# Dense query and key projections spread by transfers, maxima in a ring of three banks, and a schedule with one long piece to a slot

## The reference

```python
def _L1_attn_ref(x, w_qkv, b_qkv, w_proj, b_proj):
    ...
    q, k, v = (qkv[0], qkv[1], qkv[2])
    attn = jnp.einsum('bhqd,bhkd->bhqk', q, k) * SCALE
    attn = jax.nn.softmax(attn, axis=-1)
    out = jnp.einsum('bhqk,bhkd->bhqd', attn, v)
    ...
t = t + _L1_attn_ref(_ln_t(t), L1_attn_w_qkv, L1_attn_b_qkv, L1_attn_w_proj, L1_attn_b_proj)
t = t + _L1_ffn_ref(_ln_t(t), ...)
```

## Time and profile before

| | |
|---|---|
| Time, median of 3 runs | 249.68 us (248.03 to 251.86) |
| Profiled execution, its own time | 250.09 us |
| Its span | 248.2 us, mean granted clock 0.989 |
| PE, DVE, ACT, POOL busy | 229.0, 149.8, 118.0, 71.8 us |

### The profile page before, as it was taken

The page is one execution under the profiler, slowest core; times in us unless marked ns, Lnnn a source line. Parts: engine busy times, 40 slices in busy tenths (PEclk is TensorE's granted clock), DMA queues, the critical chain, the costliest instruction groups (busy, mean ns, idle before and its releaser), DMA issues.

```text
span 248.2 us, 5871 instructions
## 1 busy us (share of the span) xinstructions
PE 229.0 (92%) x2020; PEld 149.0 (60%) x2020; DVE 149.8 (60%) x330; ACT 118.0 (48%) x210; POOL 71.8 (29%) x117
## 2 busy tenths in 40 slices
PE   2999997989999999999889989999999999998982
PEld 2989874555557667667575564555555565644371
DVE  0129567557677678696765837566656656555183
ACT  0345056354543463463544336575756657565312
POOL 8000007000001800814510231574555546542000
PEclk9999999999999999999997999999999999999998
...
GB/s 189 228 108 121 245 276 367 358 256 248 246 81 3 3 31 0 3 33 3 198 155 0 4 46 16 49 49 50 48 48 48 48 63 48 45 51 18 93 181 127
DMA packets 25187, 25.95 MB, mean 105 GB/s; under 512 B 5900, under 2 KB 23884, under 8 KB 25164
## 3 DMA queue, kind: packets, MB, share of 16 engines
...
...
## 4 chain that ended last, share of the span: by engine, by line
PE 82%; DVE 8%; ACT 4%; DMA 3%; issue 2%; POOLq 0%
PE grid L1423 11%; PE grid L1195 9%; PE bank L1451 9%; PE grid L1430 7%; PE bank L1132 4%; PE bank L1439 4%; PE bank L1229 3%; PE bank L1211 3%; PE bank L1088 3%; PE grid L1040 3%; PE grid L1327 3%; PE bank L1135 3%; PE grid L1168 2%; PE grid L1332 2%; PE bank L1341 2%
## 5 line engine op out<-in xcount | busy, mean ns | idle before, releaser
L679 ACT ACTIVATE main<-down_all 128x576 f32 x42 | 28.5, 684 | 26.9 <-PE bank L1451 25.9
L974 DVE COPY main<-main 128x1152 f32 x41 | 31.6, 771 | 16.0 <-issue 14.1
L788 DVE TENSOR_REDUCE main<-grid 128x4 f32<-128x1024 f32 x24 | 29.3, 1223 | 18.0 <-PE grid L1168 18.0
L648 ACT ACTIVATE main<-grid 128x1024 f32<-128x1024 f32 x24 | 24.5, 1024 | 25.3 <-PE grid L1195 25.3
L517 POOL DMA_INDIRECT main<-xhat_rows,main x21 | 22.8, 1087 | 30.1 <-PE bank L1411 17.1
L1423 PE MATMUL grid<-main 128*64 128x384 f32 x160 | 29.7, 488 | 0.3 <-DVE main L958 0.3
L525 POOL DMA_INDIRECT pair_rows<-main x19 | 20.4, 1073 | 28.6 <-DVE main L964 28.6
L1168 PE MATMUL grid<-main 32*128 32x256 f32 x192 | 26.2, 400 | 1.1 <-ACT main L606 1.1
L1195 PE MATMUL grid<-main 32*128 32x256 f32 x192 | 26.1, 400 | 0.2 <-ACT main L648 0.2
L1451 PEld LDWEIGHTS bank<-main 128*64 128x64 f32 x228 | 16.1, 136 | 12.2 <-ACT main L679 8.9
L1451 PE MATMUL bank<-main 128*64 128x192 f32 x228 | 22.7, 333 | 0.0
...
## 6 DMA issues: line engine op xcount, KB each, us to landing
down_all<-wd SPq DMA_DIRECT2D x16, 288.0 KB, 4.8
...
```

The source lines that it names most:

```text
L648: act.activation(probs[:, quad % 2, 2 * (n % 2):2 * (n % 2) + 2, :, :].rearrange("p h k n -> p h (k n)"), grid[:, score_banks(n), :], ACT. ...
L679: act.activation(w_dn[:, p, h, :], dn_e(expert(t, h)), ACT.Copy).then_inc(S["w_dn_ready"], 1)
L788: vec.tensor_reduce(negmax[:, g % QUADS, :, col:col + 33:32].rearrange("p q h -> p h q"), grid[:, max_banks(n), :].rearrange("p h (q n) -> ...
L974: vec.tensor_copy(w_gu[:, p, h, :], gu_e(expert(t, h))).then_inc(S["w_gu_ready"], 1)
```

## The change

- Queries and keys of all quads but the first are projected densely: 64 columns of queries and 64 of keys in one result of 128 partitions, two quads at a time (`project_pair`). ACT evicts each into `dense`, and SP copies the rows by transfers to the even partitions of `qk_sb` (`spread_rows`), two transfers for each quad. Users wait with `wait_spread`. POOL fills the odd partitions once. The scale moves to the exponential.
- The raw weights are loaded in the dense layout, in eight transfers of short pieces, and only the first quad's are spread by DVE.
- The maxima have a ring of three banks (2, 3, 4), one bank for each head. `maxima` takes one head at a time.
- `maxima_rows` stands behind the scores of the odd slot. The second dense result and half of the values lie in bank 5 beside it, and PE waits for `shift_ready` before it writes there.
- The long pieces have slots of their own: `DENSE_AT`, `VALUES_AT`, `OUT_AT`, `TOKENS_AT`, `LOGITS_AT`.
- Expert weights are loaded in groups of experts, between the steps of `spread_rows`.

```diff
+SHIFT_ROW = 1
+WQ = 3 * 2 * C + 3 * C
+DENSE_AT = (None, 0, 3, 7, 13, 16)
+VALUES_AT = (5, 11, 17)
+OUT_AT = (9, 15, 19)
+TOKENS_AT = (14, 20)
+LOGITS_AT = (18, 21)
+RING = (2, 3, 4)
+GU_GROUPS = ((0, 3), (3, 5), (5, 8), (8, 11), (11, 13), (13, 16))
+DN_GROUPS = ((0, 4), (4, 8), (8, 12), (12, 16))
+LD_GU = 16 * 4 * len(GU_GROUPS)
+LD_DN = 16 * len(DN_GROUPS)
...
-        def out_slot(b):
-            return UNITS * (b + 1) + (1 if b == B - 2 else 2)
-        def max_banks(n):
-            i = 0 if n == 0 else 2
-            return slice(i, i + 2)
+        def max_bank(n, h):
+            return bank[h if n == 0 else RING[(2 * n + h - 2) % 3]]
         def score_banks(n):
             i = 2 if n == SPAN - 2 else 0
             return slice(i, i + 2)
-        def query_bank(m):
-            return bank[5 if m == 1 else 4][:, 0:N]
-        def key_bank(m):
-            return bank[6 if m in (1, 2) else 7][:, 0:N]
+        def dense_quads(p):
+            return [m for m in (2 * p + 1, 2 * p + 2) if m < B * QUADS]
+        def dense_bank(p, form):
+            if p == 0:
+                return bank[(5, 6)[form]][:, 0:N]
+            return bank[5][:, N:2 * N] if form else bank[7][:, 0:N]
+        def wait_spread(engine, m):
+            p = (m - 1) // 2
+            copies = sum(2 * len(dense_quads(c)) for c in range(p % 2, p + 1, 2))
+            engine.wait_ge(spread_qk[p % 2], 16 * copies)
         def value_bank(h):
-            return bank[4 if h else 7][:, 0:C]
+            return bank[5][:, N:N + C] if h else bank[7][:, 0:C]
...
-            sp.dma_start(w_raw[:, 0, :], a["w_qkv"][0:128, 0:C]).then_inc(S["ld_qkv"], 16)
-            sp.dma_start(w_raw[:, 1, :], a["w_qkv"][C - 128:C, C:2 * C]).then_inc(S["ld_qkv"], 16)
-            sp.dma_start(w_raw[64:128, 2, :], a["w_qkv"][128:C, 0:C]).then_inc(S["ld_qkv"], 16)
-            sp.dma_start(w_raw[0:64, 2, :], a["w_qkv"][0:C - 128, C:2 * C]).then_inc(S["ld_qkv"], 16)
+            for rows, m, start in ((slice(0, 128), 0, 0), (slice(0, 128), 1, C - 128), (slice(64, 128), 2, 128), (slice(0, 64), 2, 0)):
+                for part in range(2):
+                    sp.dma_start(w_d[rows, m, :, part, :], a["w_qkv"][start:start + rows.stop - rows.start, part * C:(part + 1) * C]
+                                 .rearrange("p (j n) -> p j n", j=QUADS)).then_inc(S["ld_qkv"], 16)
...
+                for part in range(2):
+                    sp.dma_start(first_bias[0:128:2, part:part + 1], a["b_qkv"][part * C:part * C + 64].unsqueeze(1)).then_inc(S["ld_qkv"], 16)
+                    sp.dma_start(dense_bias[64 * part:64 * part + 64, :],
+                                 a["b_qkv"][part * C:(part + 1) * C].rearrange("(j r) -> r j", j=QUADS)).then_inc(S["ld_qkv"], 16)
                 for r in range(4):
-                    sp.dma_start(qk_bias[32 * r:32 * r + HD, :],
-                                 a["b_qkv"][0:2 * C].rearrange("(j r d) -> r d j", r=4, d=HD)[r]).then_inc(S["ld_qkv"], 16)
...
+            def spread_rows(p):
+                for form, m in enumerate(dense_quads(p)):
+                    sp.wait_ge(S["dense_ready"], 2 * p + form + 1)
+                    if p == 0:
+                        sp.wait_ge(S["odd_rows_set"], 2)
+                    if m >= 2 * QUADS:
+                        sp.wait_ge(S["st_done"], 2 * (m - 2 * QUADS) + 2)
+                    for part in range(2):
+                        sp.dma_start(qk_sb[0:128:2, m % (2 * QUADS), part, :],
+                                     dense[64 * part:64 * part + 64, p % 2, form, :]).then_inc(spread_qk[p % 2], 16)
+            load_gate_up(*GU_GROUPS[0])
+            load_down(*DN_GROUPS[0])
+            spread_rows(0)
             sp.wait_ge(S["tok_ready"], B)
-            for e in range(BEFORE, E - LATE):
-                load_expert(e, S["ld_late"])
+            load_down(*DN_GROUPS[1])
+            load_gate_up(*GU_GROUPS[1])
+            spread_rows(1)
+            load_gate_up(*GU_GROUPS[2])
+            spread_rows(2)
+            load_gate_up(*GU_GROUPS[3])
+            spread_rows(3)
+            load_gate_up(*GU_GROUPS[4])
+            load_down(*DN_GROUPS[2])
+            spread_rows(4)
+            load_down(*DN_GROUPS[3])
+            spread_rows(5)
             sp.wait_ge(S["st_done"], UNITS * B)
-            for e in range(E - LATE, E):
-                load_expert(e, S["ld_late"])
+            load_gate_up(*GU_GROUPS[5])
...
+            pool.wait_ge(S["hid_ready"], 2 * GROUPS)
+            for part in range(2):
+                nc.gpsimd.memset(qk_sb[:, 1:, part, :], float(part)).then_inc(S["odd_rows_set"], 1)
...
-            def queries_keys(m):
-                act.wait_ge(S["qk_done"], m + 1)
-                if m >= 2 * QUADS:
-                    act.wait_ge(S["st_done"], 2 * (m - 2 * QUADS) + 2)
-                for part, src in enumerate((query_bank(m), key_bank(m))):
-                    j = part * QUADS + m % QUADS
-                    act.activation(qk_sb[:, m % (2 * QUADS), part], src, ACT.Identity, bias=qk_bias[:, j:j + 1]).then_inc(S["qk_ready"], 1)
+            def first_queries_keys():
+                act.wait_ge(S["ld_qkv"], 16 * 20)
+                act.wait_ge(S["first_done"], 1)
+                for part, src in enumerate((bank[4], bank[7])):
+                    act.activation(qk_sb[:, 0, part], src[:, 0:N], ACT.Identity, bias=first_bias[:, part:part + 1]).then_inc(S["first_ready"], 1)
+            def dense_rows(p):
+                act.wait_ge(S["dense_done"], p + 1)
+                if p >= 2:
+                    wait_spread(act, dense_quads(p - 2)[0])
+                for form, m in enumerate(dense_quads(p)):
+                    j = m % QUADS
+                    act.activation(dense[:, p % 2, form, :], dense_bank(p, form), ACT.Identity, bias=dense_bias[:, j:j + 1]).then_inc(S["dense_ready"], 1)
...
-            dve.wait_ge(S["ld_qkv"], 16 * 16)
+            dve.wait_ge(S["ld_qkv"], 16 * 20)
             dve.wait_ge(S["w_zeroed"], 6)
-            for rows, m, scale in ((slice(0, 128), 0, SCALE), (slice(0, 128), 1, 1.0), (slice(64, 128), 2, SCALE), (slice(0, 64), 2, 1.0)):
-                vec.tensor_scalar(w_qk[rows, m, :].rearrange("p (h d) -> p h d", d=32)[:, :, 0:HD],
-                                  w_raw[rows, m, :].rearrange("p (h d) -> p h d", d=HD), scale, None, ALU.mult).then_inc(S["w_spread"], 1)
-            vec.tensor_scalar(qk_bias[:, 0:QUADS], qk_bias[:, 0:QUADS], SCALE, None, ALU.mult).then_inc(S["bias_ready"], 1)
+            for rows, m, part in ((slice(0, 128), 0, 0), (slice(0, 128), 1, 1), (slice(64, 128), 2, 0), (slice(0, 64), 2, 1)):
+                vec.tensor_copy(w_first[rows, m, :].rearrange("p (x t) -> p x t", t=2)[:, :, 0],
+                                w_d[rows, m, 0, part, :]).then_inc(S["w_spread"], 1)
...
-                dve.wait_ge(S["smax_done"], n + 1)
                 if pair == 0 and g >= QUADS:
                     dve.wait_ge(S["rT_done"], g - QUADS + 1)
-                col = 64 * pair + HD
-                vec.tensor_reduce(negmax[:, g % QUADS, :, col:col + 33:32].rearrange("p q h -> p h q"),
-                                  grid[:, max_banks(n), :].rearrange("p h (q n) -> p h q n", q=2), AX.X, ALU.max, negate=True).then_inc(S["smax_ready"], 1)
+                for h in range(2):
+                    dve.wait_ge(S["smax_done"], 2 * n + h + 1)
+                    vec.tensor_reduce(negmax[:, g % QUADS, :, 64 * pair + 32 * h + SHIFT_ROW],
+                                      max_bank(n, h).rearrange("p (q n) -> p q n", q=2), AX.X, ALU.max, negate=True).then_inc(S["smax_ready"], 1)
...
-            def project_qk(m):
-                b, g = m // QUADS, m % QUADS
-                cols = slice(128 * g, 128 * g + 128)
-                dst = (query_bank(m), key_bank(m))
-                if m == 0:
-                    pe.wait_ge(S["w_spread"], 4)
-                pe.wait_ge(S["xT_ready"], max(b + 1, 2))
-                if m == 0:
-                    pe.wait_ge(S["img_ready"], 4)
-                elif m == 2:
-                    pe.wait_ge(S["xT_ready"], 3)
-                elif m > 2:
-                    pe.wait_ge(S["qk_ready"], 2 * m)
-                    pe.wait_ge(S["v_ready"], 2 * ((m + 1) // QUADS))
-                if m == 3 * QUADS:
-                    pe.wait_ge(S["x2T_ready"], 1)
-                if m > QUADS + 1 and m % QUADS == 1:
-                    pe.wait_ge(S["attn_ready"], m // QUADS - 1)
+            def project_first():
+                pe.wait_ge(S["w_spread"], 4)
+                pe.wait_ge(S["xT_ready"], 2)
+                pe.wait_ge(S["img_ready"], 4)
+                dst = (bank[4][:, 0:N], bank[7][:, 0:N])
                 for part in range(2):
-                    mm(dst[part], w_qk[:, part, cols], xT[:, b, part, :], start=True, stop=False)
+                    mm(dst[part], w_first[:, part, :], xT[:, 0, part, :], start=True, stop=False)
                 for part in range(2):
```

(72 more changed lines are left out.)

102 lines of the change are left out of this document (52 added, 50 removed).

## The result

The changed kernel took 262.59 us (median of 4 runs, 260.67 to 264.50) where the kernel before took 250.24 (median of 4): a ratio of 1.0519, with a 95% interval of 1.0461 to 1.0577. It is 12 to 13 us slower; the forecast was 249.1 and its range ended at 252.6. The profiled execution took 260.67 with a span of 258.8, against 247.6 in the forecast's sum, so 11.2 us are to be explained.

A forecast was written before the change was run, and what follows sets the result against it. PE was taken to bound the attention loop (busy 72.86 of 76.30 us). Of 7.5 us saved, waits left 1.46 gained by slot 22; less 0.9 in front, net 0.6, giving 249.1, range 246.0 to 252.6.

The forecast's parts named there:

- The front: Start of the kernel: extra weight-load issues and slower copies delay DVE's clipping, 0.9 us lost; full 2.2 a rival, 15 in 100.
- DVE's copies slowed beside POOL's fills: Start of the kernel: two POOL fills fall when DVE's copies are due and could add up to 1.2 us.
- The clock: Attention loop: new waits make the clock fall, four microseconds of matmuls at half clock giving 253; rival, 6 in 100.
- The term of the prologue: Before the loop: one projection fewer, but it lay under the first maxima's reductions; 0 to 0.2 us gained, taken as 0.
- The transfers: After dense projections: row copies land 3.9 us after D, stalling slot 15 by 1.4; late landing a rival, 7 in 100.
- D: Attention loop: PE's projection of queries and keys, 1.69 us; the mark from which the landing of its transfers is counted.
- The wait for bank 5: Odd slots: PE waits for DVE's shift of queries before dense projections or values, 5.1 us lost in all.
- the rival in which it is hidden: Odd slots: the shift is done before PE comes, so 5.1 us more are gained, giving 244.0; 8 in 100.
- Exponentials: Odd slots' scores wait for ACT to free the score banks, 6 x 0.26 = 1.6 us lost; start at E + 2.35.
- reductions: DVE in the loop: two one-bank reductions take 1.29 us where one took 1.23, lengthening its chain by 0.07.
- the 7.5 of projections: Attention loop: dense projections remove 15.21 us of PE work and add 7.73, a gain of 7.5 if nothing waited.
- E: Attention loop: the start of an even slot, from which the times of DVE and PE in a period are counted.

The follow-up runs named there:

- before_short: The kernel before, with only the change's eight transfers of 256-byte weight pieces, spread from there by DVE: 255.59 us, ratio 1.0137 to the kernel before.
- raw_early: raw_four with DVE's small copies of the first projection's weights ahead of the four long copies: 255.70 us, ratio 1.0173 to the kernel before.
- raw_four: The changed kernel with raw weights in four transfers of long rows, rearranged by DVE copies: 260.30 us, 1.032 to the kernel before by the medians.
- fill_four: The changed kernel with unused matmuls added in four places where PE waits, every wait kept: 256.89 us, ratio 1.0214 to the kernel before.
- dense_slot_11: The changed kernel with slot 13's dense projection moved to slot 11 and slot 11's values to slot 13: 256.70 us, ratio 1.0228 to the kernel before.
- two_banks: The changed kernel with heads' maxima in two banks instead of three and no PE wait for the shift: 258.66 us, ratio 1.0322 to the kernel before.

## Why the prediction was wrong

*The front, taken at 0.9 between 0 and 2.2.* This step failed first. It priced eight short-piece transfers like four long ones, at 0.55 an issue, because the row it used is of long rows; the cutting was named ("short pieces") and not priced. They took 0.81 each here, and from 0.68 to 0.92 in the seven kernels that have them: 4.33 more on the queue than the four of before, where the sum had 2.2. It then counted 0.8 of PE's reserve; the DVE start came 4.57 later, PE started the inverse 3.74 later, and a half clock on the inverse added 1.1. before_short shows 4.35 for the loads alone, raw_early that with long pieces and early copies all of it goes. The other half of the term, DVE's copies slowed beside POOL's fills, was right as a mechanism but played no part in the change, since the copies came after the fills; raw_four met it, at 1.95 more (2.69 for 0.74) where the forecast had up to 1.2.

*The clock, a rival at 6 in 100.* This step failed most. It was a rival, and the sum put it at nothing. The sum itself forecast waits of 1.4 in slots 11 and 15 and a longer idle in front, and still took all matmuls at 1.00. The waits aren't priced by their length alone: fill_four leaves every wait in, gives PE work ahead of four of them, and takes back 5.7 us, about the 5.5 that the rows at half clock cost. The term of the prologue belongs here. The dense projection that left it was put at 0, since it lay under the reductions; its length did come out at nothing, but PE now stood idle there for 1.49, and the stretch behind that idle time cost some 3 us. Slots 0 and 1 measured 7.02 at half clock and 5.13, the forecast, with it whole. The rival's own price, four microseconds of matmuls, was too low: the three stretches last 13.7, which is up to 6.8 us of matmuls at the full clock, each of which costs one more.

*The transfers, maxima of slot 15 at 3.9 after D.* The mechanism was right, the size not: they started at 103.68, 5.3 after D (98.38, the start of the next slot, as the sum counts). The last transfer landed 2.0 after its issue (median of all 22: 2.1) for my 1.8, but most of the miss were the issues: the fourth was to start 2.1 after D and started 3.2 after it, at 101.58, behind an issue of 1.35 where I counted 0.5 from start to start. PE did all the scores of the slot meanwhile (101.06 to 102.19), so that the stall shows as 1.49 only. The later start is 1.35 of the 2.7 that the period was too long; the other half is the half clock on the output projection, 3.52 for 2.12. dense_slot_11 takes back 4.0 in the two slots, the 2.7 and most of the stall that the sum had. The estimate from the Trainium skill, DMA: Bandwidth & Descriptors (Anatomy of one DMA), 2.15 for these 64 KB, agrees with the measured 2.1 better than my 1.8 does.

*The wait for bank 5* held: waits of 0.61 to 0.72 in dense and values periods and 1.41 behind statistics, periods of slots 2 to 14 within 0.25 of the forecast. These slots hold 4.2 of the sum's 5.1 for this wait and measured 4.0; the rest is due in slot 16. two_banks took it away there, and the 0.9 of waits for ACT mostly with it, and got 3.4 back. What comes next behind the wait was not priced, so the rival in which it is hidden would have given less than its 5.1.

*Exponentials, reductions, the 7.5 of projections* held: 2.35 from E to the odd slot, 1.28 for two reductions against 1.29. The gain was there and was paid out: 5 for the bank, 1.6 for the exponentials, and then the front, the clock and slot 15, which the sum had at 2.3 in all and which took some 12. The 2.3 were 0.9 for the front and 1.4 for slot 15.

What stays open: when a wait lets the clock fall. The same wait of 1.41 in slot 11 was followed by no fall in the changed kernel and by one in raw_four (low from 86.9):

```profile
86.63 1.33 PE L1216 MATMUL bank<-main 128*128 128x192 f32 x4 [1.41 <-DVE main L850]
```

The wait of slot 15 was followed by a fall in the changed kernel and, at 1.63, by none in raw_early. The kernel before waits for 1.32 ahead of its transposed maxima at 50.60, with the clock at 1.00 through the whole loop. The two kernels with places filled show that a stretch goes away when the idle time ahead of it is filled, each in one traced execution; they don't show how much idle time is needed.
